# Cross attention's scores as three fp32r products from rounded and subtracted queries and keys

## The reference, cut to what matters

```python
def _L0_xattn_ref(hidden_q, kv_c, Wq, w_kc_q, w_kc_kv, W_qr, W_kr, Wo):
    q_hk = (hidden_q @ Wq.T).reshape(Bv, Sv, H, K)
    q_big = jnp.einsum('bshk,hkq->bshq', q_hk, w_kc_q)
    q_big = _apply_rope(q_big, sin_q[None, :, None, :], cos_q[None, :, None, :])
    kv_r = _apply_rope(kv_c, sin_k[None], cos_k[None])
    q_r = jnp.einsum('bshq,hqr->bhsr', q_big, W_qr)
    k_r = jnp.einsum('bld,hdr->bhlr', kv_r, W_kr)
    scores = jnp.einsum('bhsr,bhlr->bhsl', q_r, k_r)
    attn = jax.nn.softmax(scores, axis=-1)
    ctx_c = jnp.einsum('bhsl,bld->bhsd', attn, kv_r)
    ctx_lat = jnp.einsum('bhsd,hkd->bhsk', ctx_c, w_kc_kv)
    return ctx_lat.transpose(0, 2, 1, 3).reshape(Bv, Sv, H * K) @ Wo.T

    x = x + _L0_xattn_ref(_layernorm(x), ctx_512, ...)
    x = x + _L0_attn_ref(_layernorm(x), ...)      # a second attention
    x = x + _L0_ffn_ref(_layernorm(x), ...)       # a feed-forward network
```

## Time and profile before

| | us |
|---|---|
| median of 3 runs | 1603.02 (1601.88 to 1604.45) |
| the profiled execution, its own time | 1603.56 |
| its span (first to last instruction) | 1601.4 |
| mean granted TensorE clock | 0.972 of 2.4 GHz |
| PE busy | 1485.5 (93%) |
| DVE busy | 1139.9 (71%) |
| ACT busy | 811.1 (51%) |
| POOL busy | 541.8 (34%) |

### The profile page before, as it was taken

One profiled execution on the slowest core, in us unless ns is written; L12 is line 12 of the kernel. 1 busy time (PEld: TensorE's weight loads), 2 busy tenths in 40 slices (PEclk: granted clock), 3 DMA queues, 4 the chain that ended last, 5 costly groups with the idle time before them and its releaser, 6 DMA issues. The chain is left out here.

```text
span 1601.4 us, 26509 instructions
## 1 busy us (share of the span) xinstructions
PE 1485.5 (93%) x8136; PEld 1123.1 (70%) x8136; DVE 1139.9 (71%) x1820; ACT 811.1 (51%) x1739; POOL 541.8 (34%) x594
## 2 busy tenths in 40 slices
PE   4799999999978999999999977999898899999997
PEld 3577777777746777777777766888443478787876
DVE  6888777887648788788788853777687735556466
ACT  4566565666545555555555543555211355554554
POOL 4244333442025554544545513221351202222021
PEclk9899999999989999999999988999898899999999
DMA  4223334243565444544544514000244100000000
GB/s 152 68 81 111 105 110 119 75 122 95 182 219 126 119 119 105 125 111 106 129 107 108 139 21 172 0 0 0 84 174 158 45 1 1 27 1 26 0 27 27
DMA packets 140917, 140.05 MB, mean 87 GB/s; under 512 B 84150, under 2 KB 111926, under 8 KB 139708
## 3 DMA queue, kind: packets, MB, share of 16 engines
q1 hardware_dynamic: 140284, 138.54, 30.0%
q10 hardware_dynamic: 576, 0.81, 0.2%
HBM read 109.88 MB, written 27.39 MB: 86 GB/s over the span
## 5 line engine op out<-in xcount | busy, mean ns | idle before, releaser
L997 ACT ACTIVATE c_e<-c_sc_ps,c_peak 128x257 f32<-128x257 f32 x256 | 119.6, 473 | 219.4 <-DVE c_peak L900 219.4
L878 POOL TENSOR_TENSOR c_mixed_low<-c_whole,c_mixed_high 128x512 fp32r<-128x512 f32 x64 | 81.9, 1279 | 211.0 <-ACT c_mixed_high L1017 211.0
L77 DVE TENSOR_TENSOR b_rot_parts_low<-b_rot,b_rot_parts_high 128x1536 fp32r<-128x1536 f32 x64 | 136.0, 2125 | 21.9 <-ACT b_rot_parts_high L541 21.9
L278 POOL TENSOR_TENSOR b_turned_raw<-b_turn_part 128x384 f32<-128x384 f32 x32 | 70.1, 2190 | 166.2 <-DVE b_key_parts_low L77 165.0
L1571 PE MATMUL f_ps<-f_right,f_left 128*128 128x512 f32 x256 | 115.7, 613 | 8.4 <-ACT f_raw L1614 6.1
L70 PE MATMUL c_out_ps<-c_shared_high,c_mixed_high 128*128 128x512 f32 x256 | 112.2, 438 | 11.1 <-issue 10.1
L324 DVE TENSOR_TENSOR b_rot<-b_w_qr,b_angle 128x1536 f32<-128x1536 f32 x64 | 119.2, 1862 | 0.2
L70 PE MATMUL b_ps<-c_shared_high,b_wq_parts_high 128*128 128x512 f32 x256 | 108.5, 424 | 6.5 <-DVE c_shared_low L77 6.5
L70 PE MATMUL e_mm_ps<-folded_high,e_h_t_high 128*128 128x512 f32 x256 | 106.4, 416 | 5.7 <-DVE e_h_t_low L77 5.6
L541 ACT ACTIVATE b_rot_parts_high<-b_rot 128x1536 fp32r<-128x1536 f32 x64 | 95.3, 1489 | 24.5 <-PE b_ps L72 17.0
L274 POOL TENSOR_TENSOR b_turn_part<-b_early,b_centre 128x384 f32<-128x384 f32 x64 | 82.1, 1303 | 72.2 <-DMA b_early<-early 70.5
(11 more groups left out here) (232 smaller groups left out, 3903.8 us busy)
## 6 DMA issues: line engine op xcount, KB each, us to landing
c_ends_spread<-end_weights SPq DMA_DIRECT2D x64, 256.0 KB, 4.3
carried_queries<-x SPq DMA_DIRECT2D x7, 2048.0 KB, 11.3
b_early<-early SPq DMA_DIRECT2D x15, 640.0 KB, 4.0
f_left<-ent_in SPq DMA_DIRECT2D x16, 512.0 KB, 5.4
f_right<-ent_out SPq DMA_DIRECT2D x16, 512.0 KB, 6.5
c_q_first<-carried_queries SPq DMA_DIRECT2D x32, 224.0 KB, 3.3
c_q<-carried_queries SPq DMA_DIRECT2D x32, 224.0 KB, 3.2
b_late<-late SPq DMA_DIRECT2D x16, 320.0 KB, 3.8
```

What stands on the lines that cost most here:

```text
L77: return nc.vector.tensor_tensor(low, value, high.bitcast(F32), ALU.subtract)
L878: nc.gpsimd.tensor_tensor(mixed[1][:, w, :, u], whole[:, u % 2].rearrange("p (h s) -> p h s", h=H), mixed[0][:, w, :, u].bitcast(F32), ALU ...
L997: last = nc.scalar.activation(e[:, v, c], sc_ps[:, 2 * v + c, 0:L], ACT.Exp, bias=peak[:, v, c:c + 1], accum_out=total[:, v, c:c + 1])
```

## The change

The two fp32 matmuls of a score become six fp32r products of 258 columns (keys are padded with a column of zeros, since the buffers get an even length). For that each batch's queries and keys are rounded by ACT (`round_queries`, 512 columns, and `round_keys`, 258 columns) and subtracted by POOL (`split_queries`, `split_keys`) ahead of their use: queries of b + 2 are rounded in the even step of b and subtracted in its odd step, keys of b + 2 are rounded in the odd step of b and subtracted in the even step of b + 1, ahead of the rotation.

To make room in memory, the raw keys have two buffers instead of four: the load of batch b now waits until the rotation of b - 2 is done, not that of b - 4. `c_part` moves into `spare`, so the load of the next stage's weights waits until all 64 rotations are done. The last two heads' queries of batches 0 and 1 are no longer written by ACT in `query_path`; two transfers copy them, behind the last output weights in SP's queue. The trigonometric steps of the next stage's weights (DVE) work in three parts instead of two.

```diff
+            sp.wait_ge(qc_stored, 8 * HPAIRS)
+            crossing.staged_queries(sp, staged)
...
-                    if isinstance(U, int) and U >= 2 * HPAIRS - 2:
-                        at = (H - 2 + ab) * S + base
-                        nc.scalar.activation(crossing.q[:, :, at:at + G], ps[:, QC_BANK + ab].rearrange("p (b s) -> p b s", b=B)[:, 0:2], ACT.Copy)
...
+    def staged_queries(self, sp, staged):
+        for u in range(2):
+            sp.dma_start(self.q[:, u, (H - 2) * S:].bitcast(F32), staged[:, u].rearrange("p h s -> p (h s)")).then_inc(self.q_loaded[u], 16)
...
-        part = sb("c_part", [P, 2, L])
+        part = spare[:, 0:2 * L].rearrange("p (n l) -> p n l", n=2)
...
@@ SP, one batch of a tile
-                    if known(i, 1):
-                        wait(sp, rotated_, b - BT + 1)
-                        crossing.load(sp, b, u)
                     if isinstance(b, int) and b < 2:
                         continue
+                    wait(sp, rotated_, b - 1)
+                    crossing.load(sp, b, u % 2)
                     wait(sp, scored, 2 * (b - BT) + 2)
...
             in_tiles(sp, tile)
+            sp.wait_ge(rotated_, B)
             holo.load(sp, holo_loaded)
...
@@ POOL
+            def split_queries(b, u):
+                pool.wait_ge(q_rounded, b + 1)
+                nc.gpsimd.tensor_tensor(q[u], q[u].bitcast(F32), q_high[:, u % 2].bitcast(F32), ALU.subtract).then_inc(q_split, 1)
+            def split_keys(b, u):
+                pool.wait_ge(key_rounded, b + 1)
+                nc.gpsimd.tensor_tensor(keys[1][:, u % 2], kv_even[u], keys[0][:, u % 2].bitcast(F32), ALU.subtract).then_inc(key_split, 1)
...
+                    if half == 0 and not (isinstance(b, int) and (b == 0 or b + 1 >= B)):
+                        split_keys(b + 1, (u + 1) % BT)
...
+                    if half == 1 and not (isinstance(b, int) and b + 2 >= B):
+                        split_queries(b + 2, (u + 2) % BT)
...
@@ ACT
+            def round_queries(b, u, t):
+                act.wait_ge(q_loaded[u], queries_in(u, t))
+                wait(act, scored, 2 * b - 2)
+                nc.scalar.activation(q_high[:, u % 2], q[u].bitcast(F32), ACT.Copy).then_inc(q_rounded, 1)
...
@@ PE
-                    pe.wait_ge(q_loaded[u], queries_in(u, t))
-                    pe.wait_ge(rotated_, b + 1)
+                    pe.wait_ge(q_split, b + 1)
+                    pe.wait_ge(key_split, b + 1)
...
-                    last = nc.tensor.matmul(sc_ps[:, 2 * half + c, 0:L], q[u][:, at], kv_t[u], start=True, stop=True)
+                    last = multiply_parts(nc, sc_ps[:, 2 * half + c, 0:LE], [q_high[:, u % 2, at], q[u][:, at]], [a[:, u % 2] for a in keys], True, True)
```

More of the change, by code:

```diff
@@ L691, in __init__ @@
         raw, swapped = sb("c_raw", [P, 2, L]), sb("c_swapped", [P, 2, L])
+        self.raw_pair, self.swapped_pair = raw[:], swapped[:]
         self.raw, self.swapped = ([a[:, u] for u in range(2)] for a in (raw, swapped))
-        self.q = sb("c_q_first", [P, 2, H * S])
-        self.keys = sb("c_keys_first", [P, L])
+        self.q = ctx.enter_context(nc.sbuf_tensor("c_q_first", [P, 2, H * S], F32R))
+        self.keys = sb("c_keys_first", [P, L + 1])
         self.q_loaded = [sem(f"c_q_loaded{u}") for u in range(BT)]
-        self.pool_chained, self.rotated = sem("c_pool_chained"), sem("c_rotated")
+        self.pool_chained, self.rotated, self.padded = sem("c_pool_chained"), sem("c_rotated"), sem("c_padded")
         self.table_loaded = sem("c_table_loaded")
-        self.raw_loaded = [sem(f"c_raw_loaded{u}") for u in range(BT)]
+        self.raw_loaded = [sem(f"c_raw_loaded{u}") for u in range(2)]
         self.staged_out = sem("b_staged_out")
@@ L730, in rotate_first @@
         nc.gpsimd.tensor_tensor(part[:, 1], self.swapped[0], self.table[:, 1], ALU.mult).then_inc(self.pool_chained, 1)
+        nc.gpsimd.memset(self.keys[:, L:], 0.0).then_inc(self.padded, 1)
         pool.wait_ge(self.pool_chained, 2)
-        nc.gpsimd.tensor_tensor(self.keys[:], part[:, 0], part[:, 1], ALU.add).then_inc(self.rotated, 1)
+        pool.wait_ge(self.padded, 1)
+        nc.gpsimd.tensor_tensor(self.keys[:, 0:L], part[:, 0], part[:, 1], ALU.add).then_inc(self.rotated, 1)
     def first(self, sp):
@@ L798, in queries_in @@
         def queries_in(u, t):
-            return 32 * t + (16 if u < 2 else 32)
+            return 32 * (t + 1)
         def in_tiles(engine, tile):
@@ L844, in tile @@
                              x_tiles[bass.ds(i, 1)].rearrange("t p d -> p (t d)")).then_inc(x_loaded, 16)
-            for u in range(2, BT):
-                crossing.load(sp, u, u)
             in_tiles(sp, tile)
+            sp.wait_ge(rotated_, B)
             holo.load(sp, holo_loaded)
@@ L858, in rotate @@
             def rotate(b, u, tile_of_b):
-                pool.wait_ge(raw_loaded[u], 48 * (tile_of_b + 1))
-                nc.gpsimd.tensor_tensor(part[:, 0], raw[u], table[:, 0], ALU.mult).then_inc(pool_chained, 1)
-                nc.gpsimd.tensor_tensor(part[:, 1], swapped[u], table[:, 1], ALU.mult).then_inc(pool_chained, 1)
+                pool.wait_ge(raw_loaded[u % 2], 48 * (2 * tile_of_b + u // 2 + 1))
+                nc.gpsimd.tensor_tensor(part[:, 0], raw[u % 2], table[:, 0], ALU.mult).then_inc(pool_chained, 1)
+                nc.gpsimd.tensor_tensor(part[:, 1], swapped[u % 2], table[:, 1], ALU.mult).then_inc(pool_chained, 1)
                 pool.wait_ge(pool_chained, 2 * b + 2)
@@ L1011, in round_kv, with round_keys @@
                 nc.scalar.activation(kv[0][:, u], kv_ps[:, 0:2 * P].rearrange("p (k x) -> p k x", k=2), ACT.Copy).then_inc(kv_rounded, 1)
+            def round_queries(b, u, t):
+                act.wait_ge(q_loaded[u], queries_in(u, t))
+                wait(act, scored, 2 * b - 2)
+                nc.scalar.activation(q_high[:, u % 2], q[u].bitcast(F32), ACT.Copy).then_inc(q_rounded, 1)
+            def round_keys(b, u):
+                act.wait_ge(rotated_, b + 1)
+                wait(act, scored, 2 * b - 2)
+                nc.scalar.activation(keys[0][:, u % 2], kv_even[u], ACT.Copy).then_inc(key_rounded, 1)
             def round_mixed(b, u, t, w):
@@ L1036, in tile @@
                         round_mixed(b - 1, (u - 1) % BT, i if u else i - 1, w if u else 1 - w)
+                    if not (isinstance(b, int) and b + 2 >= B):
+                        if half == 0:
+                            round_queries(b + 2, (u + 2) % BT, i + (u + 2) // BT)
+                        else:
+                            round_keys(b + 2, (u + 2) % BT)
                     if j == 3 and known(i, 2):
```

48 lines of the change are left out of this document (31 added, 17 removed).

## The result

| | before | after |
|---|---|---|
| median of the runs | 1602.99 (4 runs, 1601.88 to 1604.45) | 1660.93 (4 runs, 1660.58 to 1661.81) |
| span of the profiled execution | 1601.4 | 1659.2 |
| mean granted TensorE clock | 0.972 | 0.960 |

The ratio is 1.0362, 95% interval 1.0344 to 1.0380: 58 us slower. The forecast was 1640 with a range of 1612 to 1692. The direction, the mechanism and the range held; the loss was 58 us where the sum said 37.

The account below looks back on a forecast made before the run. The prediction took a ring of PE and DVE to bound the stage. Loop +18, start +8 and end +11 summed to +37 us on the median 1603.02, so 1640, with a range of 1612 to 1692.

Parts of the forecast that it names:

- A ring of PE and DVE: Cross attention: DVE waits for PE's score, 0.86 us, and PE for DVE; one score in a two-step ring counts.
- The gain would be 5 us, and disappears: PE's scores in the loop: 0.11 us saved over some 48 batches, swallowed by DVE's wait for the ends.
- I count nothing: POOL's added subtractions beside DVE's two-operand multiplication: one operation replaces another there, so no cost was added.
- The keys' 0.78: POOL's keys' subtraction ahead of the rotation: makes the rotation's end 0.78 us later, counted in the chain.
- SP's queue: the mis-sized term: Loop: ends leave SP after rotation and loads; two batches take 15.4 us against 14.80, +18 us in all.
- The start: Stage's start: later first queries and rotation put the first peak 5.3 us later and the first `add_end` +8 us.
- The end: Stage's end: batch 60's ends stand behind five weight loads; `add_end(60)` comes 19 us after `add_end(59)`, not 7.9: +11.
- Only the ends of the stage: Rival: loop keeps 14.8 us for two batches, only the stage's start and end cost: +14, 1617; chance 0.15.
- faster: Rival: ends land in time everywhere and each score counts, 14 less 5 at the start: 1594; chance 0.04.
- nothing measurable: Rival: ends land in time everywhere, but one score in two counts: 1603 or so; chance 0.04.
- Crowded queue: Rival: store and broadcast crowd behind loads every batch as in the first tile: +74 + 8 + 11, 1696; chance 0.12.
- POOL against DVE: Rival: POOL's queries' subtraction meets DVE's `c_e` in the odd step, up to 1.1 us a batch: +60, 1700; chance 0.03.

Follow-up runs that it names:

- e1: The changed kernel with each batch's store and broadcast of ends issued ahead of the raw keys' and queries' loads in SP's loop: 1614.06 us, ratio 1.0065 to before.
- e4: The kernel before with two raw-key buffers instead of four and SP's load waiting for the rotation of two batches before, scores unchanged: 1619.63 us, ratio 1.0107.
- e8: The changed kernel with a batch's ends issued between the raw keys' load and the queries' loads in SP's loop: 1624.42 us.
- e2: The changed kernel with the next stage's five weight loads moved behind the ends of batches 60 and 61: 1651.73 us.
- e5: The changed kernel with the SP order edits of e1 and e2 together: 1603.88 us, ratio 1.0005 to before.
- e6: As e5, with the first two batches' scores as before the change and the first queries' two heads loaded ahead of the last output weights: 1601.38 us, ratio 0.9982.
- e9: As e6, with the keys' rounding and subtraction a step earlier: 1595.51 us, ratio 0.9958 to before.
- e10: The same kernel as e6, run again beside e9: 1600.07 us, ratio 0.9982 to before.

## Why the prediction was right, and where its size was off

- **What bounds the kernel.** A ring of PE and DVE, with POOL and the ends near it: borne out by e1 (the ring is back when the ends are off the chain) and e4 (the later ends alone take over).
- **PE.** 0.71 for six products was the lower end of the forecast's 0.71 to 0.76. "The gain would be 5 us, and disappears" is what happened; its size was tested once the ends were gone: 6.3 us less in the loop of e1, net of 5 that `c_e` lost to POOL. One product comes 0.12 us after the other (0.71 / 6 = 0.118). That is the row of the same length in the earlier trace rows, 0.118, and less than the 0.127 worked out from the products of 512 columns. The formula of the Trainium skill (TensorE: Matmul & The Clock Gate, "Back-to-back issue gap") would have given 0.11 and 0.66 for the six; the same section calls it the gap of an isolated product, which under-counts short products that each load their weights, and it does so here.
- **ACT and POOL.** "I count nothing" for POOL's place was right as long as DVE waits for its ends (`c_e` 0.811 and 0.691 in the changed kernel, where it was 0.841 and 0.691) and wrong without that (0.913 and 0.709 in e1). The keys' 0.78 ahead of the rotation was counted where it belongs, in the chain; it measured 0.84 (e4 against the change). The whole link was taken as 6.90 and measured 6.70.
- **SP's queue: the mis-sized term.** Every link was as described, and four of five lengths were within 0.2. The fifth was the landing of the broadcast: 3.25 was taken, close to the least of the earlier trace rows, with the reason that nothing follows it in the queue. The median was 3.9 with nothing behind it, 3.9 in e8 with the queries' loads right behind it, 4.1 in e1 with raw keys and queries, 4.3 before the change. What is issued behind the broadcast is worth 0.4 at most, not the 1.05 that the prediction took off, and the median of the rows would have been nearer. 0.65 x 29.5 = 19 us. The rest of the 0.80 lies between landing and `add_end`, 0.27 in the mean where 0.1 was taken for the signal: in some batches `add_end` comes late by itself.
- **The start.** The first peak (+5.2) came by the path worked out: PE's first score starts at 466.38, where 466.5 was said. For the first `add_end` (+7.1) the number is right and its reason only in part, which is some luck. The sign given was a wait of 3 us for the ends; it was 0.56. Just ahead of it `c_peak` had waited 1.17 us for TensorE's scores (483.02), and the granted clock was 0.50 until 482 us, where before the change it was so until 469. With the ends off the chain (e1) the first `add_end` still comes 15.6 us behind the first peak, against 16.2 here and 14.3 before. No run separates the clock's share.
- **The end** (+9.7) came by the path worked out, with two links shorter than taken: 6.50 to the first load (7.07) and 7.15 until the broadcast goes (8.6). "After it nothing catches up" left out a loss: 1.6 us more behind `add_end(60)`. After the wait of 10 us the granted clock is 0.50 (1.2 GHz) from 976 to 984 us, and `c_peak` then waits 1.94 us for TensorE's scores, at 985.69.
- **The rivals.** "Only the ends of the stage", "faster" and "nothing measurable" all needed two batches within 14.8 us; they took 16.13. "Only the ends" needed every term at its shortest; the landing at its median was enough to rule it out. "Crowded queue" needed 10.2 us from raw load to `add_end`; it was 9.3 (3.24 + 1.91 + 4.15), halfway between this rival and the forecast's 8.4, and the total lies between both (1640 and 1696). "POOL against DVE", the queries' subtraction under way when the odd step's `c_e` begins, was not seen in the change (0.691, as before). With the ends in time (e1) it lengthens that `c_e` in 12 of 58 batches, to 0.75 to 0.81, and the mean grows by 0.02, 1 us in the loop instead of 60. The larger part of what POOL costs there is in the even step, where `c_e` meets the rotation (0.841 to 0.913): the place that the prediction had put at nothing.

The arithmetic of the whole: 7.1 + 39.2 + 9.7 + 1.6 = 57.6, and the medians differ by 57.9. Open remains why the broadcast of 256 KB takes 3.1 in one batch and 4.8 in another; no run here varied its size or its path.

## What to carry to other kernels

A transfer that leaves the moment its data is ready and is then waited for belongs ahead of prefetches in an in-order queue; when a change makes one of those prefetches wait for a later event (here by halving the buffers), everything behind it inherits the wait. When a chain of links is summed to see whether it overtakes the bound, take the median of each link, not the shortest with a reason: a chain that overtakes by 0.6 us and one that overtakes by 1.3 look much the same in a trace and differ by a factor of two in the time. And a change that looks like a loss can hide a gain: with two groups of lines moved in one queue, this one went from 3.6% slower to no difference, and with the first two batches' scores and the place of one subtraction changed, to 0.4% faster.

## What the runs showed of the hardware that was not expected

**TensorE's clock can fall behind a wait of DVE.** Before the change the granted clock was full in the whole loop. In the changed kernel, when `add_end` has waited long, TensorE pauses, and behind the pause its granted clock can fall from 2.4 to 1.2 GHz. It does so six times in the loop; the first is behind the wait of 1.35 us of batch 2 (499.33), from 502.7 to 506.1 us. The windows' columns end with the granted clock, the DMA share and GB/s:

```profile
500.00:502.00 2.00, 0.01 (x1) 0.04 (x1) 1.97 (x5) 0.94 (x2) 0.81 (x1) 1.00 0.70 169
502.00:504.00 2.00, 2.00 (x10) 1.72 (x11) 0.88 (x3) 1.52 (x6) 2.00 (x5) 0.67 0.01 0
504.00:506.00 2.00, 2.00 (x8) 1.72 (x7) 1.38 (x3) 0.78 (x2) 1.84 (x4) 0.50 0.74 162
506.00:508.00 2.00, 1.63 (x14) 1.43 (x12) 1.47 (x2) 0.74 (x3) 1.17 (x1) 0.98 0.68 201
```

The work that ends the pause, PE's first after 3.44 us without any:

```profile
501.99 0.63 PE L1117 MATMUL c_et_ps<-ident,c_e 128*128 128x128 f32 x4 [3.44 <-DVE c_e_t_low L77]
```

In the loop `add_end` waited 1.79 us or more seven times (up to 2.50). Behind five of them the clock fell, and the batch that followed took 8.3 to 8.6 us, though its own ends were in time; behind the other two (1.79 and 1.97) it stayed, and the batch took 7.5. All others take 8.0 in the mean. By these rows the clock costs 2 (five times 8.5 less 8.0) to 5 us (less 7.5) of the 39, an estimate. e2 speaks for the low end or less: the clock falls three times in its loop instead of six, and the loop takes 476.21 against 475.74. In the loops of e1 and e5, with no such waits, the clock stays full. In e6, e9 and e10 it falls two or three times between 482 and 500 us with no such wait, so late ends are not the only thing that it falls behind. A kernel that shows this part by itself wasn't tried.

**GpSimd and DVE.** Whether `c_e` (two operands in SBUF) takes 0.69 or more goes by which of the two started first. With POOL's operation under way it takes 0.71 to 1.04 in the changed kernel's 58 even steps; in the 36 odd steps in which POOL's operation starts after it, it takes 0.69, as without any. POOL's operation that starts after it is itself delayed (the rotation's second: 0.63 to 0.76 before, where `c_e` came later, and 1.08 to 1.22 behind it in the change). The Trainium skill (SBUF — State Buffer, "Who interferes with whom") says so, that the order of issue decides who is blocked; the trace agrees, 0.82 and 1.1 against 0.69 and 0.73. What had not been expected is the size: moving 0.64 us of work by one step, on an engine that is busy 41% of the time in the changed kernel, was worth 4.6 us with the same instructions.
